# First expert layer: the first rows turned and copied ahead of the second group's ranks and placing, and the second group's rows asked for three tiles later in the queue

## The chip, the cores and the metric

One program runs on one core of a Trainium2 chip. The metric is the device time of one execution in microseconds, lower is better. Engines are named as in the profile: PE (TensorE matmul), DVE (VectorE), ACT (ScalarE), POOL (GpSimd), and SP, which here only issues DMA transfers (SPq is its queue).

## What is computed

A network of four layers over 8 images of 128 channels and 16 x 16 pixels. Each layer adds a convolution-like block and then a feed-forward block, each ahead of a layer norm. The change lies in the feed-forward block of the first layer, a mixture of 8 experts with the two best experts for each of the 2048 tokens:

```python
def _L0_ffn_setup():
    B, L, D, H, E, K = (8, 2048, 128, 512, 8, 2)
...
    x = x + _L0_conv_ref(_ln_c(x), L0_conv_bias, L0_conv_up_filter, L0_conv_down_filter)
    t = _to_tokens(x)
    t = t + _L0_ffn_ref(_ln_t(t), L0_ffn_Wg, L0_ffn_W1, L0_ffn_b1, L0_ffn_W2, L0_ffn_b2)
    x = _from_tokens(t, x)
    x = x + _L1_conv_ref(_ln_c(x), L1_conv_qkv_w, L1_conv_agg_dw_w, L1_conv_agg_pw_w, L1_conv_proj_w, L1_conv_bn_gamma, L1_conv_bn_beta, L1_conv_bn_mean, L1_conv_bn_var)
```

Each token is multiplied with its expert's 128 x 512 matrix, goes through a GELU, is multiplied with the 512 x 128 matrix and is added to the residual with its normalised score as weight.

## The kernel before

The 2048 tokens are 16 token tiles of 128, in four slots of four tiles. The first expert layer works on sorted rows. The token tiles form three groups, of 4, 8 and 4 tiles (group 0, 1, 2). For each group the kernel works out how many of its token rows go to which expert and where they stand, scatters the rows to DRAM sorted by expert, loads them back, and runs them as row tiles of 128 rows with one expert each: 15, 23 and 15 row tiles, 53 in all, numbered u = 0 to 52. Group 1 is u = 15 to 37. Row tiles are treated in chunks of four (three at a group's end); chunk 3 is u = 12, 13, 14, and chunk 4 begins with u = 15.

For a group g, these steps follow one another:
- `pick_experts(g)` on DVE finds the two experts of each token.
- `ranks(g)` on PE (L852 and L854) counts the rows of each expert. `place_rows(g)` on DVE (L2031 to L2056) turns the counts into row numbers and into the expert of each row tile, and signals `rows_placed`.
- POOL scatters the rows with one indirect DMA for each token tile and choice (L646): 16 for group 1.
- `rows_in(g)` on SP (L520, L521 and L523) waits until all scatters of the group have landed and loads the rows into XG.
- `turn_rows(q)` on PE (L900) transposes a chunk into PSUM, `turned_rows(q)` on DVE (L2132) copies it to XGT, `ffn_up(u)` on PE (L911) makes the first product, ACT the GELU (L1619), and `ffn_down(u)` on PE (L925) the second.

The weights of a row tile come from DRAM by expert number, `expert_weights(u)` on SP (L505 to L509), into one of four buffers. The load for tile u + 4 waits until `ffn_down(u)` is done. Each engine works through its instructions in the order in which the code issues them. In the loop over u PE issues `ffn_up(u + 1)`, then, at the chunk's last tile but one or two, `turn_rows` of the next chunk, and then `ffn_down(u)`; for chunk 3 the turning of chunk 4 falls to u = 13:

```python
                if u == CHUNKS[q][-1] - (1 if len(CHUNKS[q]) < 4 else 2) and q + 1 < len(CHUNKS):
                    turn_rows(q + 1)
```

While the first rows are prepared, `ln_apply(1, 3)` on DVE (L1933) applies the layer norm of slot 3. PE transposes it later in `ln_turn(1, 3)` (L787), inside u = 0, and at u = 1 it makes the router's logits of slot 3 (L801), which wait for `rows_placed` of group 1.

Of the kernel before, what the change touches and what calls it, by code (L numbers as in the profile page):

```python
# [22 lines left out]
FIRST_USE = [sum(ROOM[:g]) for g in range(NG + 1)]  # L23
# [64 lines left out]
def metaformer(nc, a):  # L88
# [9 lines left out]
    with ctx:  # L98
# [96 lines left out]
        def words(pack):  # L195
            return sum(int(np.prod(shape)) for _, shape in PACKS[pack])
# [122 lines left out]
        def tile_count(u):  # L319
            return 16 * (u // 4 + 1) + (16 if u % 4 < 2 else 0)  # L320
# [26 lines left out]
        def at(count, k):  # L347

            sem, base = count
            return sem, base + k  # L350
# [140 lines left out]
        def _(sp):  # L491
# [12 lines left out]
            def expert_weights(u):  # L504
                sp.wait_ge(rows_placed, next(g for g in range(NG) if u < FIRST_USE[g + 1]) + 1)  # L505
                if u >= 4:
                    sp.wait_ge(ffn_down_done, u - 3)
                e = sp.value_load(tile_expert[0:1, u:u + 1], min_val=0, max_val=E - 1)
                sp.dma_start(WB[u % 4], a["experts"][bass.ds(e, 1)].rearrange("e p w -> (e p) w"))\  # L509
                  .then_inc(weights_in[u % 4], 16)  # L510

            def rows_in(g):
                sp.wait_ge(scattered[g], 2 * GROUPS[g][1] * 16)
                if g == 1:
                    sp.wait_ge(x_after_conv, SLOTS)
                elif g >= 2:
                    sp.wait_ge(xg_turned, FIRST_CHUNK[g - 1])
                there = rows_there[g].rearrange("(p i) c -> p i c", p=P)
                if g == 0:
                    sp.dma_start(XG[0][:, 0:4, :], there[:, 0:4, :]).then_inc(x_loaded[1], 16)  # L520
                    sp.dma_start(XG[0][:, 4:ROOM[0], :], there[:, 4:, :]).then_inc(xg_in, 16)  # L521
                else:
                    sp.dma_start(XG[g % 2][:, 0:ROOM[g], :], there).then_inc(xg_in, 16)  # L523

            def rows_out(q):
                g = CHUNK_GROUP[q]
                j, n = CHUNKS[q][0] - FIRST_USE[g], len(CHUNKS[q])
                sp.wait_ge(y_ready, q + 1)
                if q >= 1:
                    sp.wait_ge(y_stored, 16 * q)  # L530
                sp.dma_start(rows_back[g].rearrange("(p i) c -> p i c", p=P)[:, j:j + n, :],
                             YS[q % 3][:, 0:n * C].rearrange("p (i c) -> p i c", c=C)).then_inc(y_stored, 16)

            def first_experts():
                for u in range(4):
                    expert_weights(u)
                rows_in(0)
                for u in range(USES):
                    if u + 4 < USES:
                        expert_weights(u + 4)  # L540
                    if u + 6 == FIRST_USE[1]:
                        rows_in(1)
                    if u + 8 == FIRST_USE[2]:
                        rows_in(2)
                    for q in range(len(CHUNKS)):
                        if u == CHUNKS[q][-1]:
                            rows_out(q)

            for j in range(L1_CHUNKS + L2_CHUNKS):
                if j == 2:  # L550
                    first_experts()
                    sp.wait_ge(ffn_down_done, USES)
                k = j - T_RING
                if 0 <= k < L1_CHUNKS:
                    sp.wait_ge(pw_done, k + 1)
                elif k >= L1_CHUNKS:
                    sp.wait_ge(*at(conv7_done, k - L1_CHUNKS + 1))
                if j < L1_CHUNKS:
                    sp.dma_start(ring[:, j % T_RING, 0:24 * P], a["taps5"][j]).then_inc(weights_in[j % T_RING], 16)
                else:  # L560
                    sp.dma_start(ring[:, j % T_RING, :], a["taps7"][j - L1_CHUNKS])\
                      .then_inc(weights_in[j % T_RING], 16)
# [218 lines left out]
        def _(pe):  # L781
# [63 lines left out]
            def ranks(g):  # L845
                t0, n = GROUPS[g]
                bank, o = RANKS[g]
                end = o + E * (n + 1)
                pe.wait_ge(mods_in, 16)
                pe.wait_ge(experts_picked, g + 1)  # L850
                m = picked2[:, E * (t0 + g):E * (t0 + g + n + 1)]
                mm(PB[bank][:, o:end], W["rows_above"], m, start=True, stop=False)  # L852
                for k in range(1, n + 1):
                    last = mm(PB[bank][:, o + E * k:end], ones[:], m[:, 0:E * (n + 1 - k)], start=False, stop=k == n)  # L854
                last.then_inc(ranked, 1)
# [27 lines left out]
            ln_turn(1, 2, PB[6])  # L883
            logits(0, 1, 2, W["Wg0"], PB[7])
            pe.wait_ge(x_after_conv, SLOTS)
            ranks(1)

            def chunk_of(u):
                return next(q for q, c in enumerate(CHUNKS) if u in c)

            def turn_rows(q):
                g = CHUNK_GROUP[q]
                if q >= 1:
                    pe.wait_ge(xgt_ready, q)
                if q == 0:
                    pe.wait_ge(x_loaded[1], 32)
                else:
                    pe.wait_ge(xg_in, 16 * g + 16)
                for i, u in enumerate(CHUNKS[q]):
                    last = tr(PB[5][:, i * P:i * P + P], XG[g % 2][:, u - FIRST_USE[g], :], ident)  # L900
                last.then_inc(xg_turned, 1)

            def ffn_up(u):
                q = chunk_of(u)
                i = CHUNKS[q].index(u)
                pe.wait_ge(xgt_ready, q + 1)
                pe.wait_ge(weights_in[u % 4], tile_count(u))
                if u >= 3:
                    pe.wait_ge(ffn_gelu_done, u - 2)
                for hc in range(4):  # L910
                    last = mm(PB[u % 3][:, hc * P:hc * P + P], WB[u % 4][:, hc * P:hc * P + P],  # L911
                              XGT[q % 3][:, i * P:i * P + P], start=True, stop=True)
                last.then_inc(ffn_up_done, 1)
# [20 lines left out]
                last.then_inc(fb_done, 1)  # L934

            turn_rows(0)
            ffn_up(0)
            for u in range(USES):
                if u + 1 < USES:
# [948 lines left out]
        def _(dve):  # L1888
# [41 lines left out]
            def ln_apply(n, s):  # L1930
                dve.wait_ge(*at(ln_rstd[n], s + 1))
                for t in range(TILES * s, TILES * s + TILES):
                    last = v.tensor_scalar(XT[:, t, :], X[:, t, :], lnmv[:, t, 0:1], lnrs[:, t:t + 1],  # L1933
                                           ALU.subtract, ALU.mult)
                last.then_inc(xt_ready[n][0], 1)

            def router_start(r, group, tiles, bank, gamma=None):
                n = tiles.stop - tiles.start
                first = 0 if r == 2 else tiles.start
                R = lambda i: rt[:, i, tiles]  # L1940
                q = lambda i: rs1[:, i, tiles]
                lg = bank[:, E * first:E * (first + n)].rearrange("p (t e) -> p t e", t=n)
                dve.wait_ge(logits_done, 2 * SLOTS + group + 1 if r == 2 else SLOTS * r + tiles.stop // TILES)
                if gamma is not None:
                    link(v.tensor_tensor(R(2), lg, gamma.unsqueeze(1).to_broadcast([P, n, E]), ALU.add))
                    lg = R(2)
                link(v.tensor_reduce(q(0), lg, AX.X, ALU.max))
                v.tensor_tensor(R(0), lg, q(0).unsqueeze(2).to_broadcast([P, n, E]), ALU.subtract)\
                 .then_inc(router_shifted, 1)
# [172 lines left out]
            def route_start(g):  # L2122
                t0, n = GROUPS[g]
                router_start(0, g, slice(t0, t0 + n), PB[7])
                pick_experts(g)

            def turned_rows(q):
                n = P * len(CHUNKS[q])
                dve.wait_ge(xg_turned, q + 1)
                if q >= 3:  # L2130
                    dve.wait_ge(ffn_up_done, CHUNKS[q - 3][-1] + 1)
                v.tensor_copy(XGT[q % 3][:, 0:n], PB[5][:, 0:n]).then_inc(xgt_ready, 1)  # L2132
# [19 lines left out]
                ln_stats(2, s)  # L2152

            route_start(1)
            ln_apply(1, 3)
            place_rows(1)
            turned_rows(0)
            for q in range(len(CHUNKS)):
                if q + 1 < len(CHUNKS):
                    turned_rows(q + 1)  # L2160
# [569 lines left out]
```

## Time and profile before

| | us |
|---|---|
| three runs, median (lowest to highest) | 890.47 (888.15 to 892.64) |
| the profiled execution | 890.43 |
| its span in the trace | 888.6 |
| PE, DVE, ACT, POOL busy | 719.4, 568.5, 336.7, 263.1 |

The span is the stretch from the first to the last instruction of the profiled execution; some 2 us of the device time lie around it. The profiled execution lies 0.04 us off the median of the runs. A busy time is a sum over stages with different limits, so the stage of the change, from about 85 to 145 us, is read by itself.

### The profile page before, as it was taken

Reading aid. Unit: us, or ns where it says so; the run is one execution under the profiler, and the core shown is the slowest. Engines: PE = TensorE matmul, PEld = TensorE weight load, DVE = VectorE, ACT = ScalarE, POOL = GpSimd, SP = SyncE. Lnnn points to the kernel's source line nnn. Section 1 sums busy time; section 2 is a strip of 40 time slices with the busy share of each in tenths; the row PEclk is TensorE's granted clock in tenths of the full one; section 3 lists DMA queues with packets and bytes.
Section 4 is the critical chain, followed back from the end, with each engine's and each line's share of the span. In section 5 each row is a group of like instructions: output and inputs, shape, how many; then the busy total and the mean of one; then the engine's idle time right before and its main releaser. Section 6 shows DMA issues by size and latency. Waiting matters only on the chain.

```text
span 888.6 us, 13788 instructions
## 1 busy us (share of the span) xinstructions
PE 719.4 (81%) x4364; PEld 573.3 (65%) x4364; DVE 568.5 (64%) x2170; ACT 336.7 (38%) x825; POOL 263.1 (30%) x323
## 2 busy tenths in 40 slices
PE   6997589989749999988869997678775676786778
PEld 5886588988638999873348984455554453563346
DVE  7987542113343551479951034999999999989764
ACT  1000254535422222220011113788685764574321
POOL 5104332501760000020210013556555544533200
PEclk9999599999979999988979999899798999898988
DMA  9802256645620457700003300000000002002020
GB/s 346 276 1 69 66 166 203 176 152 163 217 73 1 167 207 266 262 1 0 1 0 114 136 1 0 2 1 1 1 0 1 1 1 48 1 13 48 13 48 25
DMA packets 25846, 72.64 MB, mean 82 GB/s; under 512 B 2840, under 2 KB 11032, under 8 KB 22960
## 3 DMA queue, kind: packets, MB, share of 16 engines
q1 hardware_dynamic: 23728, 67.56, 23.2%
q0 software_dynamic: 2048, 4.20, 1.6%
q8 instruction: 37, 0.61, 0.3%
q14 instruction: 33, 0.27, 0.1%
HBM read 61.61 MB, written 10.14 MB: 81 GB/s over the span
## 4 chain that ended last, share of the span: by engine, by line
PE 52%; DVE 33%; issue 6%; POOL 4%; ACT 4%; DMA 0%; DVEq 0%; POOLq 0%; ACTq 0%
PE PB L1038 6%; PE PB L911 6%; PE PB L925 5%; PE PB L1247 5%; DVE X L2327 4%; DVE arena L2578 3%; PE PB L828 3%; DVE top L2589 3%; DVE top L2573 3%; DVE arena L2592 3%; PE PB L1425 2%; PE PB L838 2%; DVE XT L1933 2%; PE PB L787 1%; POOL arena L656 1%
## 5 line engine op out<-in xcount | busy, mean ns | idle before, releaser
L779 POOL TENSOR_TENSOR arena<-arena 128x512 f32<-128x512 f32 x64 | 81.3, 1270 | 120.9 <-ACT arena L1878 120.9
L589 POOL TENSOR_TENSOR lnrs<-lnve,mhalf 128x4 f32<-128x4 f32 x20 | 20.8, 1039 | 246.4 <-DVE lnve L1916 246.1
L1334 PE MATMUL PB<-ring 128*128 128x256 f32 x256 | 76.3, 426 | 17.2 <-ACT arena L1870 16.5
L1559 PE MATMUL PB<-w_first,arena 128*128 128x128 f32 x256 | 45.6, 306 | 51.9 <-POOL arena L779 51.2
L1619 ACT ACTIVATE arena<-PB,arena 128x128 f32<-128x128 f32 x212 | 60.1, 366 | 58.5 <-PE PB L911 58.5
L1559 PEld LDWEIGHTS PB<-w_first,arena 128*128 128x128 f32 x256 | 31.9, 154 | 76.8 <-POOL arena L779 71.6
L1878 ACT ACTIVATE arena<-arena,nmx 128x256 f32<-128x256 f32 x128 | 58.2, 505 | 58.8 <-DVE arena L2592 58.4
L911 PE MATMUL PB<-arena 128*128 128x128 f32 x424 | 59.0, 284 | 13.5 <-issue 7.7
L1334 PEld LDWEIGHTS PB<-ring 128*128 128x128 f32 x256 | 48.6, 211 | 29.3 <-issue 18.8
L911 PEld LDWEIGHTS PB<-arena 128*128 128x128 f32 x424 | 53.1, 197 | 16.4 <-issue 9.4
L925 PE MATMUL PB<-ring,arena 128*128 x424 | 58.9, 283 | 0.9 <-ACT arena L1619 0.9
L1570 ACT ACTIVATE XN<-PB 128x512 f32<-128x512 f32 x20 | 11.9, 595 | 125.4 <-PE PB L787 125.4
L2573 DVE MAX8 top<-PB 128x8 f32<-128x256 f32 x128 | 48.2, 417 | 12.9 <-PE PB L1334 12.8
L1870 ACT ACTIVATE arena<-PB,nmx 128x256 f32<-128x256 f32 x128 | 53.6, 475 | 5.9 <-DVE nmx L2579 3.3
L1038 PE MATMUL PB<-arena,ring 128*128 128x128 f32 x480 | 55.7, 274 | 0.0
L925 PEld LDWEIGHTS PB<-ring,arena 128*128 128x128 f32 x424 | 53.0, 196 | 2.7 <-issue 1.6
L1038 PEld LDWEIGHTS PB<-arena,ring 128*128 128x128 f32 x480 | 54.7, 190 | 0.0
L2578 DVE MATCH_REPLACE8 arena<-top,PB 128x256 f32<-128x256 f32 x128 | 51.9, 412 | 0.0
L2592 DVE MATCH_REPLACE8 arena<-top,arena 128x256 f32<-128x256 f32 x128 | 51.3, 407 | 0.0
L646 POOL DMA_INDIRECT rows_there<-XT,row_number x32 | 31.7, 989 | 65.4 <-PE PB L911 31.0
L2589 DVE MAX8 top<-arena 128x8 f32<-128x256 f32 x128 | 47.5, 412 | 0.0
L2139 DVE COPY arena<-PB 128x512 f32<-128x512 f32 (+1 forms) x14 | 9.3, 663 | 59.4 <-PE PB L925 59.3
(327 smaller groups left out, 1599.3 us busy)
## 6 DMA issues: line engine op xcount, KB each, us to landing
ring<-in_taps_dram SPq DMA_DIRECT2D x12, 1536.0 KB, 6.9
arena<-in_experts_dram SPq DMA_DIRECT2D x53, 258.0 KB, 3.2
ring<-in_taps_dram SPq DMA_DIRECT2D x7, 1792.0 KB, 8.0
arena<-comb_rows SPq DMA_DIRECT2D x6, 512.0 KB, 6.2
w_later<-in_later_dram SPq DMA_DIRECT2D x1, 2951.5 KB, 14.3
rows_back<-arena SPq DMA_DIRECT2D x11, 256.0 KB, 3.7
ring<-in_second_dram SPq DMA_DIRECT2D x1, 2048.0 KB, 18.5
rows_there<-arena SPq DMA_DIRECT2D x2, 960.0 KB, 15.8
```

The lines of the kernel that those rows point to most:

```text
L779: g.tensor_tensor(PR[c % 2], E1[c % 2], E2[c % 2], ALU.subtract).then_inc(sub_ready, 1)
L911: last = mm(PB[u % 3][:, hc * P:hc * P + P], WB[u % 4][:, hc * P:hc * P + P], XGT[q % 3][:, i * P:i * P + P], start=True, stop=True)
L925: last = mm(PB[3 + q % 2][:, i * P:i * P + P], H[u % 3][:, hc * P:hc * P + P], W2[:, bass.ds(e * HID + hc * P, P)], start=hc == 0, stop=hc ...
L1038: last = mm(PB[[3, 6][j % 2]][:, k * P:k * P + P].rearrange("p (b y) -> p b y", b=B), ring[:, j % T_RING, (6 * k + dy) * P:(6 * k + dy) * ...
L1334: last = mm(PB[c % 2][:, q * 256:q * 256 + 256], QM[c // 2 % 3][:, o + P * q:o + P * q + P], Kc[:, N * s + HW * j:N * s + HW * j + HW], st ...
L1559: last = tr(PB[3][:, kt * 256 + q * P:kt * 256 + q * P + P], PR[c % 2][:, q * 256 + kt * P:q * 256 + kt * P + P], ident)
L1619: last = A(H[u % 3][:, hc * P:hc * P + P], PB[u % 3][:, hc * P:hc * P + P], ACT.Gelu, bias=WB[u % 4][:, HID + hc:HID + hc + 1])
L1878: last = A(E2[c % 2][:, q * 256:q * 256 + 256], REP[c % 2][:, q * 256:q * 256 + 256], ACT.Exp, bias=nmx[c % 4][:, q:q + 1])
L2573: k0 = [mark(v.max(t8[:, q, 0:8], lg[q])) for q in range(2)]
L2578: k.append(mark(v.match_replace(rp[q], t8[:, q, 0:8], lg[q], NEG)))
L2589: k2.append(mark(v.max(t8[:, q, 8:16], rp[q])))
L2592: last = v.match_replace(rp[q], t8[:, q, 8:16], rp[q], NEG)
```

## The change

It moves three calls. On PE the turning of the first chunk is issued ahead of the ranks of group 1. On DVE the copy of the first chunk is issued ahead of the layer norm of slot 3 and of the placing of group 1. On SP the load of group 1's rows is issued in the loop's pass u = 12 in place of u = 9, which is three passes later.

```diff
@@ SP, first_experts @@
                 for u in range(USES):
                     if u + 4 < USES:
                         expert_weights(u + 4)
-                    if u + 6 == FIRST_USE[1]:
+                    if u + 3 == FIRST_USE[1]:
                         rows_in(1)
@@ PE @@
             pe.wait_ge(x_after_conv, SLOTS)
-            ranks(1)
...
             turn_rows(0)
+            ranks(1)
             ffn_up(0)
@@ DVE @@
             route_start(1)
+            turned_rows(0)
             ln_apply(1, 3)
             place_rows(1)
-            turned_rows(0)
```

On PE, at the start of the expert layer, - is before and + the changed kernel; L900 of before is L899 there, and both are `turn_rows`:

```order
 L801 MATMUL PB<-w_later,XN 128x8 [waits xn_ready]
 L801 MATMUL PB<-w_later,XN 128x8 x3
-L852 MATMUL PB<-arena 128x72 [waits experts_picked,mods_in,x_after_conv]
+L899 MATMUL PB<-w_first,arena 128x128 [waits x_loaded1,x_after_conv]
+L899 MATMUL PB<-w_first,arena 128x128 x3
+L852 MATMUL PB<-arena 128x72 [waits experts_picked,mods_in]
 L854 MATMUL PB<-arena,ones 128x64
 L854 MATMUL PB<-arena,ones 128x56
```

The four transposes now wait for the first rows' load (`x_loaded1`) ahead of the ranks, and nothing but the ranks stands between them and the first `ffn_up`, which waits for the copy (`xgt_ready`).

On DVE at the same place, L2132 is the copy of a turned chunk, L1933 the layer norm of slot 3, and L2031 to L2056 the placing:

```order
 L2019 TENSOR_TENSOR comb<-rt,rs 128x64 [waits dve_step0]
-L1933 TENSOR_SCALAR XT<-X,lnmv,lnrs 128x128 [waits ln_rstd,comb_ready]
+L2132 COPY arena<-PB 128x512 [waits xg_turned,comb_ready]
+L1933 TENSOR_SCALAR XT<-X,lnmv,lnrs 128x128 [waits ln_rstd]
 L1933 TENSOR_SCALAR XT<-X,lnmv,lnrs 128x128 x3
 L2031 TENSOR_SCALAR arena<-PB 128x8 [waits ranked]
...
 L2056 CAST tile_expert<-arena 128x23 [waits dve_step0]
-L2132 COPY arena<-PB 128x512 [waits xg_turned] x2
+L2132 COPY arena<-PB 128x512 [waits xg_turned]
```

One copy has moved from behind the placing to ahead of the layer norm; the second chunk's copy stays behind the placing.

On SP, in the passes u = 9 to 13 of the changed kernel, L509 loads a tile's weights (here of tiles 15, 16 and 17), L531 stores a finished chunk, and L523 is the load of group 1's rows:

```order
L509 DMA arena<-in_experts_dram 128x516
L531 DMA rows_back<-arena 128x512 [waits y_stored,y_ready]
L508 TENSOR_LOAD tile_expert [waits ffn_down_done,rows_placed]
L508 ISA x2
L509 ISA
L509 DMA arena<-in_experts_dram 128x516
L523 DMA arena<-rows_there 128x2944 [waits x_after_conv,scattered1]
L508 TENSOR_LOAD tile_expert [waits ffn_down_done,rows_placed]
```

Before, L523 stood three weight loads and one store further up, right behind the weights of tile 13. Now it stands right behind those of tile 16, whose L508 waits for `ffn_down(12)`.

## Rows read from the trace of the kernel before

**Rows 1.** The page: span, and the chain that ended last by engine.

```profile
span 888.6 us, 13788 instructions
...
PE 52%; DVE 33%; issue 6%; POOL 4%; ACT 4%; DMA 0%; DVEq 0%; POOLq 0%; ACTq 0%
```

**Rows 2.** Timeline of PE, 94 to 109: start, duration, instructions [idle before, releaser].

```profile
94.18 0.68 PE L852 MATMUL PB<-arena 128*128 128x72 f32 x2 [5.55 <-DVE arena L2012]
94.64 3.51 PE L854 MATMUL PB<-arena,ones 128*128 128x64 f32 x16
98.01 1.09 PE L900 MATMUL PB<-w_first,arena 128*128 128x128 f32 x4
103.00 3.78 PE L911 MATMUL PB<-arena 128*128 128x128 f32 x16 [3.90 <-DVE arena L2132]
...
107.43 1.50 PE L925 MATMUL PB<-ring,arena 128*128 x8
```

**Rows 3.** Timeline of DVE, 95 to 103.

```profile
95.14 1.11 DVE L1933 TENSOR_SCALAR XT<-X,lnmv,lnrs 128x128 f32<-128x128 f32 x4
98.20 0.17 DVE L2031 TENSOR_SCALAR arena<-PB 128x8 f32<-128x8 f32 x1 [1.94 <-PE PB L854]
...
102.27 0.68 DVE L2132 COPY arena<-PB 128x512 f32<-128x512 f32 x1
```

**Rows 4.** Timeline of SP's queue: when a transfer is issued.

```profile
89.89 0.34 SPq L520 DMA_DIRECT2D arena<-rows_there  x1
...
131.73 0.34 SPq L509 DMA_DIRECT2D arena<-in_experts_dram  x1
132.17 0.37 SPq L523 DMA_DIRECT2D arena<-rows_there  x1
...
138.35 0.34 SPq L509 DMA_DIRECT2D arena<-in_experts_dram  x1
142.84 0.34 SPq L509 DMA_DIRECT2D arena<-in_experts_dram  x1
```

**Rows 5.** DMA issues, 75 to 150: count, size of each, median us to landing.

```profile
arena<-in_experts_dram SPq DMA_DIRECT2D x20, 258.0 KB, 3.6
arena<-rows_there SPq DMA_DIRECT2D x1, 1472.0 KB, 6.2
...
arena<-rows_there SPq DMA_DIRECT2D x1, 704.0 KB, 4.4
rows_there<-XT,row_number POOLq DMA_INDIRECT x27, 3.0
arena<-rows_there SPq DMA_DIRECT2D x1, 256.0 KB, 2.8
```

**Rows 6.** Timeline of POOL: first and last of group 1's 16 scatters.

```profile
102.65 1.03 POOL L646 DMA_INDIRECT rows_there<-XT,row_number  x1 [13.00 <-DVE tile_expert L2056]
...
121.66 0.96 POOL L646 DMA_INDIRECT rows_there<-XT,row_number  x1 [0.30 <-issue]
```

**Rows 7.** Timeline of PE, 136 to 142, around the turning of chunk 4.

```profile
136.40 1.06 PE L925 MATMUL PB<-ring,arena 128*128 x8
139.15 1.13 PE L911 MATMUL PB<-arena 128*128 128x128 f32 x8 [1.69 <-issue]
140.12 0.60 PE L900 MATMUL PB<-w_first,arena 128*128 128x128 f32 x4
...
140.99 1.06 PE L925 MATMUL PB<-ring,arena 128*128 x8
```

**Rows 8.** Windows: stretch, length, busy us (instructions) of PE, PEld, DVE, ACT, POOL, then PE's granted clock, DMA share, GB/s.

```profile
108.00:109.00 1.00, 1.00 (x10) 1.00 (x8) 0.00 (x0) 1.00 (x5) 0.72 (x1) 0.82 0.19 66
...
138.00:140.00 2.00, 0.85 (x7) 0.88 (x8) 0.00 (x0) 0.00 (x0) 0.00 (x0) 1.00 0.94 300
...
191.00:192.00 1.00, 0.00 (x0) 0.00 (x0) 0.00 (x0) 0.00 (x0) 0.00 (x0) 1.00 1.06 402
...
193.00:194.00 1.00, 1.00 (x9) 0.78 (x8) 0.00 (x0) 0.00 (x0) 0.00 (x0) 0.85 0.09 31
...
197.00:198.00 1.00, 1.00 (x11) 1.00 (x10) 0.61 (x1) 0.27 (x2) 0.00 (x0) 0.94 0.00 0
```

## The prediction

> **What bounds the kernel now.** I read the page first. The chain that ended last is 52% PE and 33% DVE of a span of 888.6 us [rows 1], and it runs through the stage of the change, so time taken from PE there comes off the end. Then I read the timelines of PE and DVE at the start of the expert layer. PE makes the ranks of group 1 from 94.18 to 98.15, turns the first rows by 99.10, and stands still until 103.00, released by DVE's copy L2132 [rows 2]. DVE could have made that copy early, but the code puts it behind the layer norm of slot 3 and behind the placing, which waits for the ranks and lasts from 98.20 to 102.27 [rows 3]. So the first `ffn_up` waits for work that belongs to the next group. SP's queue says that the first rows were ready long before: their 256 KB load was issued at 89.89 and took 2.8 us, so it landed near 92.7 [rows 4, 5].
>
> The second place is the hand-over from chunk 3 to chunk 4. The 1472 KB load of group 1's rows was issued at 132.17, 0.44 us behind the weights of tile 13, and took 6.2 us [rows 4, 5]: it landed near 138.4. PE turned chunk 4 at 140.12, 2.66 us after `ffn_down(12)` ended at 137.46 [rows 7]. The 1.69 us of idle there stand ahead of `ffn_up(14)` and not of L900, so the rows were in time, with 1.7 us to spare. The scatters were no limit either: the last was issued at 121.66 and such a one takes 3.0 us, so all rows stood in DRAM near 125 [rows 5, 6].
>
> **The change, part by part.**
>
> *Turning and copying early.* PE turns chunk 0 from about 92.8 and needs 1.1 us [rows 2], which fits before the ranks at 94.18, themselves released by DVE. The copy takes 0.68 us on DVE from about 95.1, right behind L2019, and pushes the layer norm of slot 3 to about 96.9. DVE idled 1.94 us ahead of the placing [rows 3], so the 0.7 us are hidden and the placing still starts at 98.20. The scatters hang on the placing and don't move. `ffn_up(0)` now follows the ranks at 98.15 in place of 103.00: **-4.85 us**. The logits of slot 3 wait for the placing at 102.3; their turn would come after `ffn_up(2)` and the turning of chunk 1, after 103, so the wait costs nothing. Should PE be so quick as to get there earlier, it waits for DVE and gives the excess back.
>
> *The clock at the start.* PE's granted clock was half until 108.36 (0.82 in the window 108 to 109 means 0.36 us at half), which is the 1.2 GHz level, and then full [rows 8]: PE was busy for 5.36 us from 103.00 before it rose. In the other case shown it fell at 193.70 and rose at 197.12, with PE busy again: 3.4 us [rows 8]. After the change PE goes from the ranks into the experts without the idle 3.9 us. If the low stretch counted from 98.15 lasts 5.4 us nothing is gained; with 3.4 us the gain is half of 2.0, so 1.0; if the ranks, busy from 94.18, count towards the rise, it comes near 99.5 and the gain is 2.0. I take **-1.0 us**, between 0 and -2.0.
>
> *The later load.* In the new order the load stands behind the weights of tile 16, which wait for `ffn_down(12)`. Those weights were issued at 138.35, 0.89 us after 137.46 [rows 4, 7], and the load follows 0.44 us behind a weight load, as at 132.17. With its 6.2 us it lands 0.89 + 0.44 + 6.2 = 7.5 us after `ffn_down(12)` ends. But the turning of chunk 4 is issued on PE right behind `ffn_up(14)`, ahead of `ffn_down(13)`, and everything behind it on PE waits too; so do ACT, the weights of tile 17 (they wait for `ffn_down(13)`) and DVE's copy. The turning thus starts 7.5 us after `ffn_down(12)` and not 2.66: **+4.9 us**, and PE stands still for about 6.4 us where it stood for 1.69. The 1.69 are no separate gain: the weights of tile 14 no longer share the engines with the big load, but the time saved only lengthens the wait behind it. Bounds of the landing: 704 KB took 4.4 and 1472 KB beside two weight loads took 6.2 [rows 5]. It will have one weight load beside it, so 5.7 is possible; on the high side a line through 256 KB in 2.8 and 704 KB in 4.4 gives 7.2. That is +4.4 to +5.9. The scatters, done near 125, hold nothing up.
>
> *The clock after the wait.* Before, PE had its full clock around 139 [rows 8]. At 191 to 192 it stood still and the clock fell at 193.70, after an idle gap less than half as long as the new one [rows 8]. So it will fall here as well. A low stretch of 3.4 to 5.4 us costs half its length where PE is the limit, 1.7 to 2.7. Part of the first tiles after it is also held by the weights of tile 17, asked for 0.8 us after `ffn_down(13)` and 3.6 us in landing [rows 5], which a half clock delays by less. I take **+2.0 us**.
>
> The Trainium skill ("TensorE: Matmul & The Clock Gate", the section on how the loop nest decides whether matmuls stay warm) gives a DMA wait ahead of matmuls as its bad pattern, after which they run cold, and so speaks against this change, as the fall at 193.70 does. The same page says in its part on the clock gate that the ramp is under 1% of a typical kernel and need not be fitted. By that remark the last term would be left out and the sum would be 1.0 us below before; by the rows it is 1.0 above.
>
> **Sum.** -4.85 - 1.0 + 4.9 + 2.0 = +1.0 us, on the profiled execution's 890.43, which is 0.04 below the median of the runs: **891.5 us**. What was won at the start is handed back at the group border. What comes later hangs on `ffn_up_done`, on the stores and on the last tile, and moves with PE one for one.
>
> **Rivals.**
>
> *The lead is kept.* The load might not hold PE up. For it: the scatters end early, SP has nothing to wait for, and PE's remaining wait before was for weights. Against it: the order rows and the 6.2 us. The gain would be 4.85 + 1.0 and up to 1.5 of the 1.69 us of idle, as the weights of tile 14 come alone: 883.1 us. It needs the load to land within 2 us of its issue, or to be issued earlier than I read. Chance 0.09.
>
> *The clock does not fall, or costs nothing.* -4.85 - 1.0 + 4.9 = -1.0: 889.5 us. For it: the weights of tile 17 might be the limit anyway. Against it: the fall at 193.70. Chance 0.12.
>
> *The lead is never there (slower).* If the first rows land late or their transposes hold up the ranks, then placing, copy and `ffn_up(0)` all wait and only the late load is left: +4.9 + 2.0 = 897.3 us. It decides for slower by over 0.5% once less than 2.4 of the 4.85 us are gained. The load would have to land 2.4 us later than 92.7 plus the 0.3 us of slack; nothing in the queue suggests that. Chance 0.06.
>
> *The low clock lasts longer.* After the wait it would have to last 10.9 us, twice the longer case shown, to carry the sum past 0.5%: 895 us. Chance 0.06.
>
> *The forecast.* Chance 0.67.
>
> **How the numbers follow.** A measurement of this kernel can tell about 0.5%, 4.45 us, from no change. The forecast's own range puts the bounds together: 889.7 (clock gain 2.0, landing 5.7, low stretch 3.4) to 894.1 (0, 7.2, 5.4). A clock fall such as that at 193.70, worth 1.7 us, may appear or vanish elsewhere when the stages shift by a microsecond, and the runs of before spread by 2.2 us to either side. So 887.0 to 895.0 for eight in ten. Same: the forecast and the unfallen clock, 0.79, as few of their values pass 4.45 us. Faster 0.10: the kept lead and a tail. Slower 0.11: its two cases, less what of them stays inside.
>
> **What the profile of the changed kernel would show.** L2132 at about 95.1 and the first `ffn_up` right behind the ranks at about 98.2; `rows_placed` and the first scatter unchanged at about 102.6; `ffn_down(12)` ending near 131.6; L523 issued about 1.3 us later and landing near 139.1; PE idle for about 6.4 us ahead of the turning of chunk 4, which starts near 139.1 against 140.12; then a granted clock of 0.5 for 3 to 5 us. The prediction is wrong if the idle time ahead of that turning is under 3 us, if the clock stays at 1.0 behind it, or if the first `ffn_up` does not start before 100.

## The result and the profile after

The changed kernel took 893.53 us (median of 20 runs, 890.22 to 904.91), the kernel before 890.9 us (20 runs, 886.79 to 900.29). The ratio is 1.004 with an interval of 1.0022 to 1.0057: by the ratio 3.6 us slower. That is clear of noise and inside the 0.5% (4.45 us) that was called "same", though the upper end of the interval lies a little above it. The ratio leaves one disturbed execution of the changed kernel (904.91) out. The quotient of the medians, 1.003 or 2.6 us, lies inside the interval too. The profiled execution took 894.08 us.

The page of the changed kernel, span, clock by slices and the chain by engine:

```profile
span 892.3 us, 13789 instructions
...
PEclk9999797999969999988979999899897898798988
...
PE 50%; DVE 27%; issue 10%; POOL 8%; ACT 4%; DMA 1%; DVEq 0%; SPq 0%; POOLq 0%; ACTq 0%
```

The span is 3.7 us longer. In the chain of [rows 1] DMA had 0%; now it has 1%, and "issue" has grown from 6% to 10%.

The timeline of PE after, at the start of the expert layer, answers to [rows 2]:

```profile
92.97 1.09 PE L899 MATMUL PB<-w_first,arena 128*128 128x128 f32 x4 [4.04 <-DMA arena<-rows_there]
94.49 0.67 PE L852 MATMUL PB<-arena 128*128 128x72 f32 x2 [0.43 <-DVE arena L2012]
94.96 3.51 PE L854 MATMUL PB<-arena,ones 128*128 128x64 f32 x16
98.32 3.73 PE L910 MATMUL PB<-arena 128*128 128x128 f32 x16
101.88 0.61 PE L787 MATMUL PB<-w_first,XT 128*128 128x128 f32 x4
102.32 1.06 PE L924 MATMUL PB<-ring,arena 128*128 x8
```

The first `ffn_up` (L910) stands right behind the ranks, with no idle time, at 98.32 where it was at 103.00. The whole trace runs 0.31 us later at this point (the ranks at 94.49 in place of 94.18), so the lead by itself is 4.99 us. `ffn_down(0)` ends at 103.38 where it ended at 108.93: 5.55 us, of which 0.87 us are the clock.

DVE after, answering to [rows 3]:

```profile
95.46 0.69 DVE L2132 COPY arena<-PB 128x512 f32<-128x512 f32 x1
96.07 1.11 DVE L1933 TENSOR_SCALAR XT<-X,lnmv,lnrs 128x128 f32<-128x128 f32 x4
98.51 0.17 DVE L2031 TENSOR_SCALAR arena<-PB 128x8 f32<-128x8 f32 x1 [1.33 <-PE PB L854]
```

The copy is hidden: DVE's idle time ahead of the placing shrank from 1.94 to 1.33 us and the placing starts when the ranks allow it.

SP's queue and PE at the group border, answering to [rows 4] and [rows 7]:

```profile
132.14 0.37 SPq L531 DMA_DIRECT2D rows_back<-arena  x1
133.53 0.34 SPq L509 DMA_DIRECT2D arena<-in_experts_dram  x1
133.97 0.37 SPq L523 DMA_DIRECT2D arena<-rows_there  x1
146.10 3.92 SPq L509 DMA_DIRECT2D arena<-in_experts_dram  x2
```

```profile
131.63 1.05 PE L924 MATMUL PB<-ring,arena 128*128 x8
132.52 1.06 PE L910 MATMUL PB<-arena 128*128 128x128 f32 x8
141.65 1.08 PE L899 MATMUL PB<-w_first,arena 128*128 128x128 f32 x4 [8.08 <-DMA arena<-rows_there]
142.53 1.06 PE L807 MATMUL PB<-w_first,comb 128*8 128x128 f32 x4
143.39 1.91 PE L924 MATMUL PB<-ring,arena 128*128 x8
145.09 1.61 PE L910 MATMUL PB<-arena 128*128 128x128 f32 x8
146.64 1.15 PE L931 MATMUL PB<-arena 8*128 8x128 f32 x8
147.72 1.16 PE L924 MATMUL PB<-ring,arena 128*128 x8
```

`ffn_down(12)` ends at 132.68, 4.78 us ahead of before. The load is issued 1.29 us later, and PE then stands still for 8.08 us, released by the transfer of `rows_there`. That wait did not exist before. The 1.69 us ahead of `ffn_up(14)` are gone, as the forecast said they would be, without being a gain: it starts at 132.52 behind `ffn_down(12)`, with the big load no longer beside its weights. Nothing else is issued on SP for 12 us, since the next weights wait for `ffn_down(13)`, which is queued behind the turning.

The windows of the changed kernel around the wait, columns as in [rows 8], and the load's row (KB, us to landing), which answers to [rows 5]:

```profile
136.00:137.00 1.00, 0.00 (x0) 0.00 (x0) 0.00 (x0) 0.00 (x0) 0.00 (x0) 0.51 0.96 332
...
140.00:141.00 1.00, 0.00 (x0) 0.00 (x0) 0.00 (x0) 0.00 (x0) 0.00 (x0) 0.50 0.11 47
...
145.00:146.00 1.00, 1.00 (x7) 1.00 (x7) 0.00 (x0) 0.21 (x1) 0.00 (x0) 0.50 0.00 0
146.00:147.00 1.00, 1.00 (x8) 0.88 (x8) 0.00 (x0) 0.26 (x1) 0.00 (x0) 0.87 0.10 16
```

```profile
arena<-rows_there SPq DMA_DIRECT2D x1, 1472.0 KB, 7.5
```

The granted clock fell at 136.0, while PE stood still, and rose at 146.26. From 141.65 PE worked 4.6 us at the 1.2 GHz level. The way from the turning to the start of `ffn_down(14)` took 6.07 us (141.65 to 147.72) and before 3.83 us (140.12 to 143.95). The last part of the landing is thin: from 140 to 141 the DMA engines are busy for 0.11 of the time. At the start of `ffn_down(14)` the changed kernel is 3.77 us behind. The end of the span shows 3.7 us, but the lag is not constant on the way there: in between, at the start of the transposes of L787, it is 3.20 (259.59 against 256.39). The fall of the clock at 193.70 of before is not there; in the changed kernel it falls at 187.2 and rises at 190.6.

### The profile page after: what moved, and what is told of

The parts are those of the page before. It is cut to its first block, busy times and chain, and to the rows that moved or that the text cites. A ratio compares the mean times of both kernels' runs of the same rounds, so it can differ in the third digit from the quotient of the medians.

```text
span 892.3 us, 13789 instructions
## 1 busy us (share of the span) xinstructions
PE 725.4 (81%) x4364; PEld 577.9 (65%) x4364; DVE 569.9 (64%) x2170; ACT 336.8 (38%) x825; POOL 263.2 (29%) x323
## 4 chain that ended last, share of the span: by engine, by line
PE 50%; DVE 27%; issue 10%; POOL 8%; ACT 4%; DMA 1%; DVEq 0%; SPq 0%; POOLq 0%; ACTq 0%
PE PB L1038 6%; PE PB L910 5%; PE PB L1247 5%; PE PB L924 5%; DVE X L2327 4%; POOL arena L779 3%; PE PB L828 3%; PE PB L1425 3%; DVE arena L2578 2%; DVE top L2589 2%; DVE top L2573 2%; DVE arena L2592 2%; PE PB L838 2%; DVE XT L1933 2%; POOL arena L656 2%
## 5 line engine op out<-in xcount | busy, mean ns | idle before, releaser
L1334 PE MATMUL PB<-ring 128*128 128x256 f32 x256 | 79.3, 439 | 16.4 <-ACT arena L1870 15.8
L910 PE MATMUL PB<-arena 128*128 128x128 f32 x424 | 60.2, 288 | 9.3 <-issue 7.3
L910 PEld LDWEIGHTS PB<-arena 128*128 128x128 f32 x424 | 54.6, 202 | 11.4 <-issue 8.4
```

Source lines behind the costliest of these rows:

```text
L1334: last = mm(PB[c % 2][:, q * 256:q * 256 + 256], QM[c // 2 % 3][:, o + P * q:o + P * q + P], Kc[:, N * s + HW * j:N * s + HW * j + HW], st ...
```

## The experiments

**Where the load stands.** Four kernels take the two parts of the change apart. Three keep the early turning and copying and differ in one number:

```diff
-                    if u + 3 == FIRST_USE[1]:
+                    if u + 6 == FIRST_USE[1]:
                         rows_in(1)
```

This is early_u9; early_u10 has `u + 5` there and early_u11 `u + 4`. The fourth, late_only, is the kernel before with `u + 3` in that line.

early_u9: 

> The early turning and copying alone, with the load of group 1's rows left at u = 9. Theory (the move of the load costs all that the early copy wins): ffn_up(0) starts 4.7 to 4.9 us earlier as in the changed kernel, the load is issued near 127 and has landed by about 134, the turning of chunk 4 starts near 135 against 140.12 before, with PE's clock at full level around it; the time is 4.5 to 5.5 us below before, about 885.5, ratio 0.994. Rival (the early order itself is what costs, or its lead is absorbed at the group border by the load or the scatters whatever the load's place): no better than the kernel before, 890 to 894, ratio 1.000 to 1.004.

late_only: 

> The load of group 1's rows moved to u = 12 alone, PE and DVE in their order of before. Theory: the turning of chunk 4 starts 8.9 us after ffn_down(12), 6 us later than before, behind an idle PE, and the clock behind it is low for 3 to 5 us: +7 to +9 us, 898 to 900, ratio 1.008 to 1.010. Rival (the late load is harmless and the reordering costs): 890 to 892, ratio 1.000 to 1.002.

early_u10: 

> Early turning, load issued at u = 10, behind the weights of tile 14. Theory: the load is issued near 129, lands near 136, and the turning starts near 136.5 behind 2 to 3 us of idle PE; -3.5 us where the clock stays up, -1.5 where it falls: 887 to 889, ratio 0.996 to 0.998. Rival (place of the load does not matter): the same time as with u = 12, ratio 1.004.

early_u11: 

> Early turning, load issued at u = 11, behind the weights of tile 15. Theory: issued near 132, lands near 139.5, turning near 139.7 behind about 5.5 us of idle PE, and the clock falls: -0.4 + 2.2, so +1.8 us against before, 892.5, ratio 1.002. Rival (place of the load does not matter): ratio 1.004.

Times are in us; "landing" is the time from issue to landing.

| kernel | ratio to before (interval) | load issued | landing | PE idle at the border | turning of chunk 4 |
|---|---|---|---|---|---|
| before | 1 | 132.17 | 6.2 | 1.69 | 140.12 |
| early_u9 | 0.9921 (0.9884 to 0.9959) | 126.42 | 6.2 | 1.87 | 135.06 |
| early_u10 | 0.994 (0.9903 to 0.9976) | 127.98 | 6.7 | 2.48 | 134.79 |
| early_u11 | 0.9989 (0.9957 to 1.0021) | 131.76 | 6.5 | 5.18 | 138.38 |
| changed, u = 12 | 1.004 (1.0022 to 1.0057) | 133.97 | 7.5 | 8.08 | 141.65 |
| late_only | 1.0062 (1.0031 to 1.0092) | 139.07 | 7.2 | 7.75 | 146.43 |

The early order alone gains, and the late load alone costs. The rival, that the reordering is what hurts or that its lead is lost at the border whatever the load does, falls with both. Between u = 10 and u = 12 the idle time grows by 2.7 and 2.9 us for each pass of the loop. Three sizes were off: late_only came out at +0.6% where +0.8 to 1.0% was expected, early_u11 at no difference where +0.2% was expected, and early_u10 at -0.6% where -0.2 to -0.4% was expected. All three expected values touch the intervals.

The timelines of PE of early_u9 and of late_only at the border:

```profile
130.44 1.06 PE L924 MATMUL PB<-ring,arena 128*128 x8
133.37 1.90 PE L910 MATMUL PB<-arena 128*128 128x128 f32 x8 [1.87 <-issue]
135.06 1.06 PE L899 MATMUL PB<-w_first,arena 128*128 128x128 f32 x4
```

```profile
137.62 1.06 PE L911 MATMUL PB<-arena 128*128 128x128 f32 x8
146.43 1.09 PE L900 MATMUL PB<-w_first,arena 128*128 128x128 f32 x4 [7.75 <-DMA arena<-rows_there]
```

In early_u9 the idle time stands ahead of `ffn_up(14)` and not of the turning: as before, the turning is not held up by the rows. That it is a wait for weights the profile does not say (it gives "issue"); early_split_apart, below, bears on it. In late_only it stands ahead of the turning and is released by the transfer.

**Which of the moved calls makes the lead.** copy_early_only is the kernel before with the DVE copy alone moved; PE and SP are as before.

```diff
             route_start(1)
+            turned_rows(0)
             ln_apply(1, 3)
             place_rows(1)
-            turned_rows(0)
```

> The kernel before with the DVE copy of chunk 0 alone moved ahead of the layer norm and the placing; PE still turns the rows behind the ranks, and the load stays at u = 9. Theory (the lead is the placing's time on DVE, and the early turning on PE is what keeps the placing from being pushed back): the copy runs near 99.3, ffn_up(0) starts near 100.0, 3.0 us earlier than before, but the layer norm and the placing end 2.8 us later and so do the scatters; about 3 us under before, ratio 0.997. Rival (the moved copy gains all by itself, PE's order is idle): as early_u9, ratio 0.992.

Ratio 0.9961 (0.9927 to 0.9995), as expected; the interval overlaps that of early_u9, so it is the traces that tell the two apart. Its timelines of PE and DVE:

```profile
93.27 0.67 PE L852 MATMUL PB<-arena 128*128 128x72 f32 x2 [5.55 <-DVE arena L2012]
93.74 3.52 PE L854 MATMUL PB<-arena,ones 128*128 128x64 f32 x16
97.10 1.09 PE L900 MATMUL PB<-w_first,arena 128*128 128x128 f32 x4
99.05 3.78 PE L911 MATMUL PB<-arena 128*128 128x128 f32 x16 [0.85 <-DVE arena L2132]
...
136.00 1.13 PE L911 MATMUL PB<-arena 128*128 128x128 f32 x8 [3.07 <-issue]
```

```profile
98.30 0.69 DVE L2132 COPY arena<-PB 128x512 f32<-128x512 f32 x1 [4.11 <-PE PB L900]
98.91 1.10 DVE L1933 TENSOR_SCALAR XT<-X,lnmv,lnrs 128x128 f32<-128x128 f32 x4
99.94 0.15 DVE L2031 TENSOR_SCALAR arena<-PB 128x8 f32<-128x8 f32 x1
```

This execution is 0.9 us early from the layer before (the ranks start at 93.27), so distances from the ranks are compared. The first `ffn_up` starts 5.78 us behind them in place of 8.82: a lead of 3.04 us, as expected. The placing starts 6.67 us behind them in place of 4.02, so it is pushed back by 2.65 us, and the scatters with it. The load at u = 9, issued at 128.46, then has waited 0.8 us for the last scatters; the weights of tile 14 are issued 1.1 us behind it and share the engines with it, and PE idles 3.07 us. The early turning on PE is thus worth 2 us of lead (4.99 less 3.04), and it keeps the placing where it was.

**The low clock by itself.** Two kernels put matmuls of constants ahead of the turning of chunk 4 in the changed kernel; their result is not used.

```diff
+                    if q + 1 == FIRST_CHUNK[1]:
+                        for _ in range(28):
+                            mm(PB[7][:, 256:384], ones[:], ident, start=True, stop=True)
                     turn_rows(q + 1)
```

This is late_filled; late_filled_longer has 38 in place of 28.

late_filled: 

> The changed kernel with 28 matmuls of constants (128x128, about 6.2 us of PE at full clock) put ahead of the turning of chunk 4, so that PE is busy for most of its 8.1 us wait; their result is not used. Theory (the low clock behind the wait costs about 2.2 us on its own): the turning starts at the same time, 141.6, the granted clock stays at 1.0, and the following ffn_down(14) starts about 2.2 us earlier than in the changed kernel: about 891.5, ratio to before 1.001. Rival (behind the wait the weights of tile 17 are the limit, the clock costs nothing): ratio 1.004 as for the changed kernel.

late_filled_longer: 

> As late_filled, with 38 matmuls in place of 28 (about 8.4 us of PE), so that PE is busy up to the landing of the rows; in late_filled 2.45 us of idle were left behind the filling and the clock fell all the same. Theory (the low clock costs about 2.2 us on its own): clock at 1.0 behind the turning of chunk 4, the ffn_down(14) of the loop starts 3.8 us behind the turning as in the kernel before, where it took 6.1 us in the changed kernel; about 2 us under the changed kernel, ratio to before 1.001 to 1.002. Rival (the weights of tile 17 are the limit there): 6 us from the turning to ffn_down(14) with the clock at 1.0, ratio 1.004.

late_filled missed its aim. The filling ended at 138.6, the load took 8.2 us, and behind the 2.45 us of idle left the clock fell all the same (the window 141 to 142 shows 0.63, that of 144 to 145 0.66). Its ratio of 1.0039 (0.9993 to 1.0085) tells nothing about the clock's price. The longer filling left 0.47 us. PE of late_filled_longer:

```profile
132.52 8.65 PE L945 MATMUL PB<-w_first,ones 128*128 128x128 f32 x76
141.64 0.63 PE L899 MATMUL PB<-w_first,arena 128*128 128x128 f32 x4 [0.47 <-DMA arena<-rows_there]
142.10 0.60 PE L807 MATMUL PB<-w_first,comb 128*8 128x128 f32 x4
...
145.80 1.16 PE L924 MATMUL PB<-ring,arena 128*128 x8
...
149.48 0.60 PE L899 MATMUL PB<-w_first,arena 128*128 128x128 f32 x4
```

One window of it, columns as in [rows 8]:

```profile
145.00:146.00 1.00, 1.00 (x9) 0.88 (x9) 0.00 (x0) 0.97 (x4) 0.45 (x1) 1.00 0.32 52
```

The turning starts at 141.64, as in the changed kernel (141.65), and the granted clock is 1.00 from 140 to 152. `ffn_down(14)` follows 4.16 us later in place of 6.07, and the turning of chunk 5 starts at 149.48 in place of 151.40. The low clock thus costs 1.9 us in this place. In the timing, 1.0026 (0.9998 to 1.0054) lies on the expected side of 1.004 but is not told from it; the price rests on the two traces. Nor does it show at the end of this execution: its span is 892.4 us as against 892.3, the lead of 1.92 us at chunk 5 having shrunk to 0.99 by the same transposes of L787 (258.60 against 259.59) and gone later. So 1.9 us is what the clock costs in this place, and how much of it reaches the end is not shown.

**The size of the load.** late_split and early_split divide it into the four row tiles of chunk 4 and the other 19, issued one behind the other; late_split does so at u = 12 and early_split at u = 9; early_split_apart issues the first at u = 9 and the rest at u = 12. PE's wait ahead of chunk 4 is then for the first part alone.

```diff
+                elif g == 1:
+                    sp.dma_start(XG[1][:, 0:4, :], there[:, 0:4, :]).then_inc(x_loaded[2], 16)
+                    sp.dma_start(XG[1][:, 4:ROOM[1], :], there[:, 4:, :]).then_inc(xg_in, 16)
...
+                elif q == FIRST_CHUNK[1]:
+                    pe.wait_ge(x_loaded[2], 32)
```

late_split: 

> The changed kernel with the load of group 1's rows still behind the weights of tile 16, but in two transfers: the four row tiles of chunk 4 (256 KB) first, and the other 19 behind it, as group 0's load is made. Theory (PE waits for the transfer's landing): the first part lands 2.6 to 3 us after its issue near 134, the turning starts near 137, PE's wait falls from 8.1 to about 3.5 us; 886.5 to 889, ratio 0.995 to 0.998. Rival (the issue's place and not the size is the cost; the two parts share the engines and land together): turning at 140 to 141, ratio 1.002 to 1.004.

Ratio 0.9981 (0.9949 to 1.0014). The first part took 4.6 us and not 2.6 to 3, and the second, issued 0.42 us behind it, 7.1 us; the turning started at 138.97 behind 5.10 us of idle. Both views hold a part: splitting won 2.7 us of the 4.6 expected. That the first part was slowed by the second sharing the engines is not shown: in the kernel before, group 0's first 256 KB took 2.8 us with 704 KB issued 0.37 us behind it, and here the store and the weights of tile 16 were issued 1.8 and 0.45 us ahead. The median, 888.64, is at the expected place, but the turning is not, and the profiled execution took 893.92 us; that timing is no confirmation. Its interval reaches from the expected values almost to the rival's.

early_split: 

> Early turning, load at u = 9, in the same two transfers, one right behind the other. Theory: the rows of chunk 4 are early, but the second transfer still shares the engines with the weights of tile 14, PE idles 1.5 to 2 us ahead of ffn_up(14), and the time is that of the unsplit load at u = 9: ratio 0.991 to 0.994. Rival (the turning waited for the rows there): 0.5 to 1 us faster than unsplit.

Ratio 0.9948 (0.9918 to 0.9978). PE idled 1.19 us ahead of `ffn_up(14)`, less than the 1.5 to 2 expected, and the turning started at 134.19. The time is not told from that of early_u9.

early_split_apart: 

> Early turning; the four row tiles of chunk 4 are loaded at u = 9, the other 19 at u = 12, behind the weights of tile 16. Theory (at the border it is the big load beside the weights of tile 14 that makes PE idle 1.7 to 1.9 us and its clock fall): idle ahead of ffn_up(14) under 0.7 us, turning of chunk 4 near 133.5, clock at 1.0 around it, 1.5 to 3 us below the unsplit load at u = 9: 883.5, ratio 0.989 to 0.991. Rival (that idle time has another cause, or the rest of the rows is then late for chunk 5): ratio 0.992 or more.

Ratio 0.9932 (0.9897 to 0.9966). PE of early_split_apart:

```profile
131.78 1.06 PE L917 MATMUL PB<-arena 128*128 128x128 f32 x8
132.67 0.60 PE L906 MATMUL PB<-w_first,arena 128*128 128x128 f32 x4
...
140.82 1.13 PE L917 MATMUL PB<-arena 128*128 128x128 f32 x8 [1.37 <-issue]
```

The idle time ahead of `ffn_up(14)` is gone, the clock stays at 1.00, and the turning starts at 132.67. That it was the big load beside the weights of tile 14 is shown: the idle time also goes in late_only and in the changed kernel, where the load is issued later. The time, however, missed the 0.989 to 0.991 that was expected and lies in the rival's range of 0.992 or more, though the interval covers both. And 1.37 us of idle appear ahead of `ffn_up(17)`, whose weights are in flight together with the second part. The two best were run side by side once more:

early_u9_again: 

> The early turning and copying with the load at u = 9 once more, beside the split version on one chip. Expected: ratio 0.992 to 0.995.

early_split_apart_again: 

> The split version (four row tiles at u = 9, the rest at u = 12) beside early_u9_again on one chip. Theory (its border is 1.5 to 2.4 us shorter in the trace, part of which the weights of tiles 17 and 18 give back, being loaded beside the second part): 0.5 to 1.5 us below early_u9_again. Rival (all of it is given back): the same time within 0.3 us.

Ratios 0.9957 (0.9924 to 0.9989) and 0.9951 (0.9921 to 0.998), medians 885.98 and 885.78. The medians are 0.2 us apart, as the rival says, but intervals of some 3 us to either side do not exclude a gain of 0.5 to 1.5 us. No gain of the split is shown; its 1.36 us of idle ahead of `ffn_up(17)` stand again in this trace. In early_u9_again the idle time ahead of `ffn_up(14)` was 1.43 us and the clock stayed at 1.00, where 1.87 us in early_u9 went with a fall at 133.54. The simple version beats both kernels, by 0.4 to 0.8% against before.

## Why the prediction was right, and where its sizes were off

**The early order.** Right in mechanism and size: -4.85 forecast, -4.99 measured with the trace's own shift taken out, the copy hidden on DVE and the scatters unmoved (first one 8.48 us behind the ranks, before 8.47). The clock at the start gave 0.87 us where 1.0 was taken: it rose at 101.88.

**The lead on its way to the border.** The forecast carried 5.85 us to `ffn_down(12)`; 4.78 arrived. 0.31 us is the later start of this execution. The rest, 0.8 us, went mostly into waits for weights and for the copy of chunk 2 (PE idle 1.14 us ahead of `ffn_up(12)` where 0.72 stood, 1.90 ahead of `ffn_up(8)` where 1.75 stood). That all later work hangs rigidly on PE was the assumption that was slightly wrong. How much arrives also varies between executions: counted from the start of the ranks, `ffn_down(12)` ended 5.1 us earlier than before in the changed kernel and in early_u9, and 5.5, 5.9 and 6.1 us earlier in early_u11, early_u9_again and early_u10, whose PE order up to there is the same.

**The later load.** This is the term that was mis-sized most: +4.9 forecast, +6.3 measured (8.97 us from the end of `ffn_down(12)` to the turning, against 2.66). The issue came at 1.29 us as forecast (1.33). The landing took 7.5 us where 6.2 was taken and 7.2 was the upper bound (the line through the two smaller loads gives 7.14, not 7.2).

**The clock after the wait.** +2.0 forecast, +2.24 measured between the turning and `ffn_down(14)`, and 1.9 us of it shown to be the clock by late_filled_longer. The rule of the Trainium skill ("TensorE: Matmul & The Clock Gate", on the loop nest), that a DMA wait ahead of matmuls lets them run cold, holds here with that price. The Trainium skill's remark on the same page, in its part on the clock gate, that the ramp is under 1% of a typical kernel agrees in size, as 1.9 us are 0.2% of this span. But to leave the term out for that reason would have left out about half of this change's whole effect.

**The sum.** +1.0 forecast, +3.77 in the trace at `ffn_down(14)`, +3.6 in the timing. The difference is 1.4 us of the later load, nearly all of it landing, 1.1 us of lead, and 0.2 to 0.3 us of clock. The rival of a lead that never comes is excluded by the first `ffn_up` at 98.32; the kept lead (-7.35 us) would have been near had the load stayed where it was: early_u9 gained 7.0 us by its ratio, its repeat 3.8.

So the mechanism was right, and the time was closer to the edge than the sum says. The parts missed by 2.7 us together, almost all to the slow side. The measured 3.6 us stand against a bound of 4.45, and the profiled landings of the same load at u = 12 reached 8.4 us: 0.9 us more would have brought the sum to the bound. That "same" held was in part luck.

## What to carry to other kernels

In this kernel a transfer's place in the issuing queue was fixed by what its predecessors wait for. Each pass of the loop was worth 2.7 to 2.9 us of delay, and a load that was 1.7 us early at u = 9 kept PE waiting for 8 us at u = 12. Before moving a load later to clear the way for others, count from the event that releases the instruction ahead of it to the landing, and compare with the first consumer on the in-order engine; what stands behind that consumer waits as well. And two edits that are timed together should be timed apart: this change held a gain of 4 to 7 us (early_u9 and its repeat) and a loss that ate it.

## What the runs showed of the hardware that was not expected

The same 1472 KB load landed in 6.2 to 6.3 us when it was issued at u = 9 (before, early_u9, early_u9_again; 6.7 in copy_early_only), in 6.5 to 6.7 at u = 10 and 11, and in 7.2 to 8.4 at u = 12 (late_only 7.2, changed 7.5, late_filled 8.2, late_filled_longer 8.4), though fewer weight loads run beside it there. At u = 12 it is issued 1.8 us behind the store of a finished chunk, which at u = 9 to 11 comes after it. The 1216 KB part of the split load leans the same way: 5.6 us at u = 9 (early_split), 7.0 and 7.1 at u = 12 (early_split_apart_again, late_split). Whether the store is the cause was not tried and stays open. Most of the load is in earlier than its landing says: in the changed kernel the share of the DMA engines falls to 0.11 in the window 140 to 141, and in late_filled, whose turning starts at 141.07, to 0.08 and 0.03 in the windows 139 to 140 and 140 to 141.

The idle time that goes with a fall of the clock varied: 2.45 us in late_filled and 1.87 us in early_u9 went with one, 1.43 us in early_u9_again and 1.69 us in the kernel before did not. The fall did not always come in the idle time: in early_u9 it came 0.17 us after PE had started again, and in late_split, behind 5.10 us of idle, 0.2 us after. In the changed kernel it also fell at 187.2 without a gap: PE was busy for 0.95 to 1.00 us in each window from 183 to 187, in which it ran the 16 matmuls of one column of L966 (184.98 to 186.82); in the kernel before the same matmuls at 181.17 had no fall behind them. Whether these matmuls are the cause was not tried. The low stretch lasted 3.4 us; at half the clock that is an estimated 1.7 us of PE that one execution has and another has not. How much of the spread of the runs comes of it was not measured.
